# Causal attention over 32 groups with expert tiles between its scores: bursts of 4, 3, 3 banks, one block of value products, row maxima turned at full width and stacks loaded one group at a time

## The reference, cut to what matters

```python
q = (x @ wq).reshape(bsz, seq_len, N_HEADS, HEAD_DIM)
k = (x @ wk).reshape(bsz, seq_len, N_KV_HEADS, HEAD_DIM)
v = (x @ wv).reshape(bsz, seq_len, N_KV_HEADS, HEAD_DIM)
...
scores = jnp.einsum('bqhd,bkhd->bhqk', q, k) / np.float32(np.sqrt(HEAD_DIM))
scores = scores + mask
attn = jax.nn.softmax(scores.astype(jnp.float32), axis=-1).astype(q.dtype)
out = jnp.einsum('bhqk,bkhd->bqhd', attn, v).reshape(bsz, seq_len, N_HEADS * HEAD_DIM)
...
y_all = jax.nn.relu(jnp.einsum('bsd,edh->bseh', x, W_e) + b_e)
```

## Time and profile before

| | |
|---|---|
| runs of before | 664.77, 665.72, 666.27 us, median 665.72 |
| profiled execution | span 663.2 us; the page gives no time around it |
| PE busy in the span | 627.2 us (95%) |
| DVE busy in the span | 552.0 us (83%) |
| stretch from T of group 2 (137.80) to T of group 31 (543.09) | 405.3 us for 29 groups, 13.98 each |

### The profile page before, as it was taken

The page is one execution under the profiler, slowest core; times in us unless marked ns, Lnnn a source line. Parts: engine busy times, 40 slices in busy tenths (PEclk is TensorE's granted clock), DMA queues, the critical chain, the costliest instruction groups (busy, mean ns, idle before and its releaser), DMA issues.

```text
span 663.2 us, 12226 instructions
## 1 busy us (share of the span) xinstructions
PE 627.2 (95%) x3565; PEld 338.9 (51%) x3565; DVE 552.0 (83%) x1788; ACT 287.0 (43%) x535; POOL 238.2 (36%) x364
## 2 busy tenths in 40 slices
PE   8999999998999999999999999999999999789997
PEld 5788784433433334433443344443444343478886
DVE  6698999869978888989888798897789975689994
ACT  4353325434434435444444444443455443444441
POOL 3777641333323212332221322322222115576620
PEclk9999999969989999999999999999999999899999
DMA  7599989889788564675954649667276527768842
GB/s 262 141 336 266 337 239 173 146 164 273 152 268 161 166 139 80 154 132 188 194 105 98 136 109 220 125 173 152 52 167 111 171 72 241 156 145 217 217 104 79
DMA packets 79902, 113.10 MB, mean 171 GB/s; under 512 B 9704, under 2 KB 42664, under 8 KB 79840
## 3 DMA queue, kind: packets, MB, share of 16 engines
q1 hardware_dynamic: 68098, 86.90, 53.5%
q0 software_dynamic: 6704, 18.62, 11.8%
q10 hardware_dynamic: 5038, 6.84, 4.2%
HBM read 72.15 MB, written 39.65 MB: 169 GB/s over the span
## 4 chain that ended last, share of the span: by engine, by line
PE 55%; DVE 25%; DMA 8%; issue 4%; SPq 3%; POOL 2%; ACT 1%; ACTq 0%; DVEq 0%; POOLq 0%
PE bank L1672 13%; DVE bank L1390 12%; PE bank L1023 8%; PE bank L1591 7%; PE bank L2162 6%; PE bank L1644 5%; PE bank L1683 4%; PE bank L2167 4%; DMA w_e<-expert_rows,slots 3%; PE bank L1617 3%; DVE arena L1390 2%; DMA qt<-arena 2%; DMA qt<-turned_parts 2%; DVE m_parts L1403 2%; DVE m_parts L1405 1%
## 5 line engine op out<-in xcount | busy, mean ns | idle before, releaser
L1390 DVE CUSTOM_DVE_ANT_0 bank<-bank,cst 128x384 f32<-128x384 f32 (+3 forms) x512 | 234.9, 521 | 47.6 <-PE bank L1591 44.5
L1514 ACT ACTIVATE arena<-bank 128x512 f32<-128x512 f32 x320 | 170.9, 599 | 180.2 <-PE bank L1617 149.7
L1332 POOL TENSOR_SCALAR_AFFINE_SELECT arena<-arena 128x512 f32<-128x512 f32 x128 | 80.7, 643 | 309.2 <-ACT arena L1514 309.2
L1672 PE MATMUL bank<-w_e,arena 128*128 x312 | 162.2, 626 | 0.0
L1591 PE MATMUL bank<-kt,qt 48*128 48x512 f32 (+1 forms) x496 | 111.0, 338 | 5.6 <-DVE arena L1390 5.0
L1591 PEld LDWEIGHTS bank<-kt,qt 48*128 48x128 f32 x496 | 70.1, 187 | 83.9 <-DVE arena L1390 51.7
L1617 PE MATMUL bank<-qt,kt 50*128 50x512 f32 x256 | 88.2, 452 | 2.4 <-DMA qt<-arena 2.0
L1644 PE MATMUL bank<-arena 128*32 128x512 f32 (+3 forms) x1024 | 84.8, 445 | 0.4 <-ACT arena L1514 0.4
L1672 PEld LDWEIGHTS bank<-w_e,arena 128*128 128x128 f32 x312 | 54.6, 193 | 58.0 <-issue 54.3
L1390 DVE DVE_READ_ACCUMULATOR2_ANT arena<- 128x1 f32 x512 | 71.9, 140 | 0.0
L1683 PE MATMUL bank<-w_proj,arena 128*128 128x512 f32 x128 | 67.6, 636 | 0.0
(11 more groups left out here) (167 smaller groups left out, 942.7 us busy)
## 6 DMA issues: line engine op xcount, KB each, us to landing
qt<-turned_parts SPq DMA_DIRECT2D x96, 128.0 KB, 4.7
turned_parts<-qk_parts SPq DMA_DIRECT2D x8, 1280.0 KB, 7.2
gathered_rows<-s_tok SPq DMA_DIRECT2D x39, 256.0 KB, 5.3
arena<-gathered_rows SPq DMA_DIRECT2D x39, 256.0 KB, 3.4
expert_rows<-arena SPq DMA_DIRECT2D x39, 256.0 KB, 4.5
w_e<-in_L_ffn_W_e ACTq DMA_DIRECT2D x24, 256.0 KB, 6.2
kt<-turned_parts SPq DMA_DIRECT2D x96, 64.0 KB, 4.4
arena<-in_L_attn_x SPq DMA_DIRECT2D x16, 256.0 KB, 6.1
```

The source lines that it names most:

```text
L1332: g.affine_select(out=diag, in_=diag, compare_op=ALU.is_ge, fill=0.0, base=0, pattern=[[0, 2], [0, HALF], [1, P]], channel_multiplier=-1). ...
L1390: i = v.tensor_tensor_reduce(out=part, in0=part, in1=const("mask")[:, S - w:], scale=1.0, scalar=LOWEST, op0=ALU.add, op1=ALU.max, accum_o ...
L1514: nc.scalar.activation(pt[:, s, first:second + 1:second - first].rearrange("p c r q -> p c (r q)"), s2_bank(b, h, n).rearrange("p (c x) -> ...
L1672: i = t.matmul(bank[7], xgt[:, m % 2, k * P:(k + 1) * P], w_e[:, ex[m], k, :], start=False, stop=(k == KB - 1))
```

## The change

1. Four gaps instead of five; the quarters stand 2, 2, 2 or 2, 4, 2 or 4, 2, 2, and none in the last gap. TensorE's list of a group is now: scores 3 to 6 of the next group beside 0 to 3 of this one, gap 0, scores 7 to 9 beside 4 to 6, gap 1, T, scores 0 to 2 of the group after the next beside 7 to 9, gap 2, all four value products.
2. The row maxima are not split first. One copy puts them, twice, into the first two eighths of each half of `m_cols` (128 x 128, the rest zero from the start); T turns all 128 columns into bank 4; VectorE then makes the high part of the turned rows (a copy of 128 x 128) and, with a constant column that is -1 on the low rows and 0 elsewhere, high and low part in one more instruction. The constant rows of `kt` are -1 instead of 1. T also waits for `rows_of` of the last group, and the first value product for the read of bank 4.
3. Both row DMAs are issued by SP.
4. `load_stack` brings one group's stack with eight DMAs, four groups ahead of the group in work (before: twelve for two groups, three ahead).
5. `turns()` places `expert_x` by a new rule. In the groups 3 to 29 it stands at the first place of a group five times (18 times before) and twice at the second place of nine groups (never before).

```diff
-GAPS = 5
+GAPS = 4
-SIX, EIGHT = (2, 1, 1, 1, 1), (2, 2, 1, 1, 2)
+SIX, MIDDLE, FRONT = (2, 2, 2, 0), (2, 4, 2, 0), (4, 2, 2, 0)
-SIZES = [NONE, (0, 0, 0, 2, 2)] + [SIX, EIGHT] * 12 + [SIX, SIX] + [SIX, EIGHT, (2, 2, 1, 1, 0), NONE]
+SIZES = [NONE, (0, 0, 2, 2)] + [SIX, MIDDLE, SIX, FRONT] * 6 + [SIX, SIX] + [SIX, MIDDLE, SIX, NONE]
...
-        t = first[m] - 2 + m if m < 2 else max(first[m] - 2, last[m - 2])
-        t += -1 if t % 2 == 0 and (m < 2 or t > last[m - 2]) else t % 2 == 0
...
+        free = last[m - 2] if m > 1 else GAPS
+        slots = [t for t in range(free, first[m]) if t % GAPS in (1, 2)]
+        t = max([t for t in slots if t < first[m] - 1] or slots)
...
+    put("less", -1.0 * (p // 8 % 8 == 1))
...
-            if due(at := nth_of(NJ, b, h, -2 * NJ)):
+            if due(at := nth_of(NJ, b, h, -3 * NJ)):
                 e.wait_ge(b_s2, at)
...
-            for s in range(2):
-                for piece, (of_q, of_k) in enumerate(((0, 0), (0, 1), (1, 0))):
-                    at = 64 * s + HD * piece
-                    if (b, h) != (0, 0):
-                        e.dma_start(kt[at:at + HD, buf].bitcast(F32), k_rows[of_k]).then_inc(b_ld[buf], 16)
-                    e.dma_start(qt[at:at + HD, buf].bitcast(F32).rearrange("i g r t -> i g (r t)"), q_rows[of_q, s]).then_inc(b_ld[buf], 16)
+            for s in range(2):
+                at = 64 * s
+                if b or h > 1:
+                    e.dma_start(keys[at:at + 2 * HD].bitcast(F32), k_rows).then_inc(loaded, 16)
+                    e.dma_start(keys[at + 2 * HD:at + ROWS].bitcast(F32), k_rows[0]).then_inc(loaded, 16)
+                e.dma_start(queries[at:at + HD].bitcast(F32).rearrange("i r t -> i (r t)"), q_rows[s, 0]).then_inc(loaded, 16)
+                e.dma_start(queries[at + HD:at + ROWS].bitcast(F32).rearrange("i r t -> i (r t)"), q_rows[s]).then_inc(loaded, 16)
...
+        def maxima_columns(e, b, h):
+
+            e.wait_ge(b_m, nth_of(NJ, b, h, NJ))
+            rows = row_max.rearrange("p (s r) t -> p s (r t)", s=2)
+            nc.vector.tensor_copy(m_cols[:, :, 0:2], rows.unsqueeze(2).to_broadcast([P, 2, 2, HALF * TPB])).then_inc(b_mx, 1)
...
-            nc.vector.tensor_copy(m_rows, S1_BANK[nth_of(NJ, b, h, NJ + 2) % 3][0:2 * 2 * HALF * TPB, 0:P]).then_inc(b_me, 1)
+            v.tensor_copy(m_high[:, :], turned_at(b, h)).then_inc(dve_steps, st.one())
+            e.wait_ge(dve_steps, st.count())
+            v.scalar_tensor_tensor(out=m_rows[:, :], in0=m_high[:, :].bitcast(F32), scalar=const("less"), in1=turned_at(b, h),
+                                   op0=ALU.mult, op1=ALU.add).then_inc(b_me, 1)
...
-                    if b * NG + h + 1 < NB * NG:
-                        maximum_rows(e, *next_group(b, h, 1), 1)
-                    for n in (8, 9):
-                        exps(e, b, h, n)
-                    results(b, h, 3, 4)
+                    results(b, h, 2, 3)
...
-                    scores(e, (2, 3, 4), following, (0, 1, 2), (b, h))
+                    scores(e, (3, 4, 5, 6), following, (0, 1, 2, 3), (b, h))
                     quarters(b, h, 0)
-                    scores(e, (5, 6, 7), following, (3, 4, 5), (b, h))
+                    scores(e, (7, 8, 9), following, (4, 5, 6), (b, h))
                     quarters(b, h, 1)
-                    scores(e, (8, 9), following, (6, 7), (b, h))
-                    values(e, b, h, 0)
+                    turn_maxima(e, *following)
+                    scores(e, (0, 1, 2), after, (7, 8, 9), (b, h))
                     quarters(b, h, 2)
-                    turn_maxima(e, *following)
-                    scores(e, (0, 1), after, (8, 9), (b, h))
+                    for j in ORDER:
+                        values(e, b, h, j)
                     quarters(b, h, 3)
-                    for j in ORDER[1:]:
-                        values(e, b, h, j)
-                    quarters(b, h, 4)
...
-                        maximum_rows(e, *next_group(b, h, 1), 0)
-                    if h % 2 and b * NG + h + 3 < NB * NG:
-                        load_stacks(e, *next_group(b, h, 3))
+                        for s in range(2):
+                            maximum_rows(e, *next_group(b, h, 1), s)
+                    if b * NG + h + 4 < NB * NG:
+                        load_stack(e, *next_group(b, h, 4))
```

More of the change, by code:

```diff
@@ L77, in times_of @@
 def times_of(k):
-    return {UNITS[n][1]: 4 * (b * KV + h) + min(gap, 3) for (b, h, gap), quarters in WORK.items() for n, q in quarters
+    return {UNITS[n][1]: GAPS * (b * KV + h) + gap for (b, h, gap), quarters in WORK.items() for n, q in quarters
             if q == k and UNITS[n][0] == "x"}
@@ L121 @@
 for _name, _n in (("ident", P), ("half", 1), ("eps", 1), ("minus", 1), ("mask", S), ("tri", P), ("cos", TPB * 8), ("sin", TPB * 8), ("s4", 16),
-                  ("lower", E * E), ("i128", NT), ("i128m", MT + 1), ("tile", MT), ("iota", P), ("tilenum", TOPK * NT), ("part", 1), ("sel", E)):
+                  ("lower", E * E), ("i128", NT), ("i128m", MT + 1), ("tile", MT), ("iota", P), ("tilenum", TOPK * NT), ("part", 1), ("sel", E), ("less", 1)):
     COLS[_name] = (_at, _at + _n)
@@ L460, in sp_a @@
                         load_first(e)
-            load_stacks(e, 0, 0)
+            for h in (0, 1):
+                load_stack(e, 0, h)
         def dve_a(e, st):
@@ L466, in dve_a @@
             v.memset(be3[:, :], 0.0).then_inc(dve_steps, st.one())
+            v.memset(m_cols, 0.0).then_inc(dve_steps, st.one())
             e.wait_ge(a_load, 16)
@@ L622, in dve_a @@
                 maxima(e, 0, 1, n)
-            maxima_parts(e, st, 0, 1)
-            maxima_rows(e, 0, 1)
+            maxima_columns(e, 0, 1)
+            maxima_rows(e, st, 0, 1)
             dve_experts(e, st)
-            for n in (0, 1):
+            for n in (0, 1, 2):
                 maxima(e, 0, 2, n)
@@ L1070, in pe_a @@
                 values(e, 0, 0, j)
-            scores(e, (0, 1), (0, 2), (), None)
+            scores(e, (0, 1, 2), (0, 2), (), None)
             keep_awake(6, bank[2])
@@ L1207, in build @@
         row_max = take([P, R, TPB])
-        m_parts = parts("m_parts", [P, 2, 2, HALF * TPB], "arena", used[0])
-        take([P, 2, 2, HALF * TPB])
-        m_rows = take([P, P])[0:2 * 2 * HALF * TPB]
+        m_cols = take([P, 2, 8, HALF * TPB])
+        m_high = parts("m_high", [P, P], "arena", used[0])
+        take([P, P])
+        m_rows = parts("m_rows", [P, P], "arena", used[0])
+        take([P, P])
         rsum = take([P, QB])
@@ L1371, in build, with first_half, turned_at @@
         LOWEST = -3.0e38
-        def first_half(n):
-            return (n + 1) % 2, n // 2
+        def first_half(b, h, n):
+            return (n + (b * NG + h < 2)) % 2, n // 2
+        def turned_at(b, h):
+            return bank[(0, 1)[h] if b * NG + h < 2 else 4][:, 0:P]
         def maxima(e, b, h, n):
             v = nc.vector
-            s, kind = first_half(n)
+            s, kind = first_half(b, h, n)
             if n == 0 and due(at := nth_of(1, b, h, 0)):
@@ L1465, in go @@
                     if following:
-                        for n in (2, 3, 4):
+                        for n in (3, 4, 5, 6):
                             maxima(e, *following, n)
@@ L1472, in go @@
                     if following:
-                        for n in range(5, NJ):
+                        for n in (7, 8, 9):
                             maxima(e, *following, n)
-                        maxima_parts(e, st, *following)
+                        maxima_columns(e, *following)
                     for m in TURNS.get((b, h, 0), ()):
@@ L1478, in go @@
                     if following:
-                        maxima_rows(e, *following)
+                        maxima_rows(e, st, *following)
                     if after:
-                        for n in (0, 1):
+                        for n in (0, 1, 2):
                             maxima(e, *after, n)
@@ L1576, in scores_1 @@
             elif n == 0:
[L1577 to L1580 removed]
+                e.wait_ge(b_ld[h % 4], 16 * LOADS * (2 * b + h // 4 + 1) - (16 * LOADS // 2 if h % 4 < 2 else 0))
+            if n == 2 and b == 0 and h in (1, 2):
+                e.wait_ge(b_me, h)
             if (b, h) == (0, 1) and n == 0:
@@ L1819, in sp_b @@
                 load_expert(e, x)
-            load_stacks(e, 0, 2)
+            for h in (2, 3):
+                load_stack(e, 0, h)
             for b in range(NB):
```

61 lines of the change are left out of this document (24 added, 37 removed).

## The result

The changed kernel takes 708.4 us (median of 4 runs, 706.7 to 710.8) where the kernel before takes 665.25 beside it: 1.065 of before, 95% interval 1.062 to 1.069. The prediction was 664.1, range 654 to 673. It was wrong by 44 us.

The account below looks back on a forecast made before the run. PE was taken to set the pace, busy 388.0 of 405.3 us, with DVE 60 us to spare. The terms -20.9, -3.4, +16.8, +9.9 and -4.0 sum to -1.6 us, so 665.7 becomes 664.1 us, range 654 to 673.

Parts of the forecast that it names:

- item 5: Stack loads: eight issues a group instead of twelve in two, and a longer lead; worth nothing, SP's queue has room.
- Item 6: Both row DMAs on SP, one behind the other: the second lands in time unless queues are full; counted as 0.
- rival B: Slower, chance 0.25: rows, issued behind store and expert tiles, come too late for `scores_2(0)`; 9 us, 670 in all with 6.
- the landing of the rows sets the bursts: Sign that the prediction is wrong: row DMAs' landing, not the fourth bank's wait for maxima, sets the bursts; no size given.
- Rows as releasers of `scores_2(0)`: Sign in the new profile, at the head of the burst of four, that would show the rival with late rows.
- The lead-in "at nothing": Before T of group 2: one more row DMA on its chain, a shorter way to T; counted at nothing with the tail.
- The tail "at nothing": Behind T of group 31: a quarter and a value product more, fewer ahead; counted at nothing with the lead-in.
- rival D: Slower, chance 0.10: DVE's work behind T is longer; PE holes of 2 us or more in groups 3, 4, 21 lower the clock.
- Items 1 to 4: PE's work -20.9 us, wait at T -3.4, fourth bank of a burst +16.8, DVE late there +9.9, scores' old waits -4.0.
- item 2: T's wait for maxima falls from 14.1 to 10.7 us, -3.4; loads before a shape change always idle 0.76.

Follow-up runs that it names:

- E5: Changed kernel, still eight stack transfers a group, but with the 16 rows as outermost dimension and the 2 parts inside; 669.2 us, 1.006 of before.
- E3: Kernel before, its twelve stack transfers for two groups replaced by the changed kernel's eight for each group, at the same place; 840.1 us, 1.262 of before.
- E2: Changed kernel with the loads of before: two groups at once in 12 transfers of 16 partitions, three groups ahead; 703.7 us, 1.059 of before.
- E12: Kernel before with only its stacks loaded per group, four groups ahead, in 8 transfers with the rows outermost; 662.4 us, 0.994 of before.
- E9: E5 with row transfers ahead of gap 1's store and the expert tiles behind groups 11 and 19 alone; 666.3 us, 1.000 of before.
- E10: E5 with the nine doubled `expert_x` split, one at a place, the first of each pair one place earlier; 662.3 us, 0.995 of before.
- E7: Changed kernel, keys' 32-partition transfers (64 KB, 2 a group) kept, queries' cut in two of 16; 670.9 us, 1.008 of before.
- E1: Changed kernel, each stack transfer of 32 partitions cut in two of 16, so 12 transfers a group instead of 8; 670.8 us, 1.007 of before.

## Why the prediction was wrong

**The step that failed is item 5.** It said "eight DMA issues a group instead of twelve in two groups" and "more lead is worth nothing". It counted transfers and did not read their shape. Four of the eight have an outermost dimension of 2 and 3 updates each instead of 16, and while only a load's transfers moved the DMA share was 0.12, two of the 16 engines. Setting that right brings back 39 us of 43 (E5), and doing it to the kernel before costs 175 us (E3). "More lead is worth nothing" was read from a row of before (0.2 us of waiting for stacks), and that row does not show how little room there was: before, the last update of a load came less than 0.7 us ahead of the next T, or behind it, in 9 of 15 loads. With the old lead and the old pairs the new order takes 704 us (E2), since its load starts later behind T and its groups are shorter. Which of the two harms, and whether the longer lead was needed once a load lands in 7 us, is open. And in the old order loading per group is worth 4 us (E12), which the prediction had at nothing too.

**Item 6, counted as 0, and rival B** had the right place and a wrong reason. One of the prediction's own signs of being wrong, that the landing of the rows sets the bursts, came true. Rows as releasers of `scores_2(0)` are in the profile, 21.6 us on PE, also in plain groups like 13, where B has none. B's mechanism (issue behind the store and tiles) is real and is worth 2.4 us once landings are sound (E9). B was priced at a landing of 3.7 us, which no row shows; the 5.47 us of the earlier trace rows would have given (3.2 + 5.47 - 5.9) x 7 = 19 us, and its second term, 0.4 x 5, is 0.2 x 5 by its own numbers. The 5.47 us row was read as a full queue. A landing time depends on the shapes in flight (the same row transfer lands 5.4 us behind its issue in group 13 of the changed kernel and 2.0 in E5), and the change had altered these.

**The lead-in "at nothing"** cost 15.7 us, for the same cause: E5's T of group 2 stands at 137.0, 0.8 us ahead of before. **The tail "at nothing"** is 2.7 us longer in E5 (122.8 against 120.1), with the gathers of expert weights on its chain from 9.6 us behind T of group 31 on, 7.8 before. This was not tested by itself.

**The clock** (rival D's second half). In the stretch the granted clock is 0.96 where before has 0.99; of 430.9 us that is some 13 us more lost. It is at 0.5 of full speed in eight separate stretches of 3.4 us, besides one that T of group 2 stands in, as in every kernel here. Five of the eight begin within 2.5 us behind a wait of `scores_2(0)` for rows (0.80 to 4.05 us long), one (185.9) behind a wait of 2.06 us for maxima in a burst of four, two (274.7 and 387.3) behind a wait of T of 1.57 us for maxima. In E5, with nearly none of the waits for rows, there are two, behind waits of 2.38 and 1.79 us for maxima in groups 3 and 21, two of the three that D had named. So most of it is a second cost of the same cause: PE's waits for rows (16.6 us in the stretch against 2.5 in all of E5) and the clock (4% of 430.9 against 2% of 405.0, 9 us) make 23 of the 25.9 us between the changed kernel and E5. D, and with it the range up to 673, counted up to 1.7 us for each such stretch. No run shows this term by itself: it is an estimate, half of the 3.4 us at 0.50 that the earlier trace rows has once, behind 1.32 us of idle time on PE.

**Items 1 to 4 held**, and with the loads repaired the forecast is nearly met: E5's stretch is 405.0 against 405.3 before, where the sum said -1.6. (E5's trace is of an execution of 666.6 us; the median of its runs is 669.2, 5 over the forecast.) In single terms, from E5's order of time: `scores_2(0)` at T + 5.37 (said 5.37); the last pair of the burst of four 1.35 behind the first (said 1.34), the burst 1.78 us (said 1.77); groups with six quarters 12.4 (said 12.4), the h = 0 groups 13.7 (12.4 + 1.37), those with eight 13.8 to 14.5 where nothing disturbs them (said 13.7 and 14.1). T's weight load idles 29.5 us (said 33). (The 0.76 us of the earlier trace rows is in the trace of before the least idle time of a load of scores or values behind quarters, 116 of them; in front of quarters behind scores the median is 0.15, so item 2's "always" holds for the first alone.) The split of the rows takes 0.59 us from T's read to the next maximum (said 0.61). The bursts of four are 64.8 - 51.3 = 13.5 us over their 29 x 1.77; 2.5 of that are the two waits for rows, which leaves 11.0 for the lateness of VectorE (said 9.9). E10 shows that the doubled `expert_x` makes 3.7 of it.

## What to carry to other kernels

Before a load is called equivalent, read the outermost dimension of both its access patterns, not its bytes or its count: 2 there held the DMA share at 0.12, two of the 16 engines, with 192 KB a group for each of them by that reading, and 16 there with the same bytes brought back 39 of the 43 us (E5). It shows in a trace as updates of the semaphore per transfer (3 instead of 16) and as other transfers that land late in places that were not touched. And no wait in the old order does not mean that there is room: work out when a tile is wanted, when its buffer is free and how long its load takes to land, in the new order, before the row of the old one is believed.

## What the runs showed that was not expected

- The harm is not in proportion to the bytes: 64 KB a group on each of the two engines cost nothing (E7), 192 KB cost 38 us (changed kernel against E1), and 384 KB in one go every second group 175 us (E3). The last landing comes 9.0, 13.2 and 22.0 us behind the first issue, and a group lasts 12.4 to 14.1. In E3 the stacks themselves are waited for (145.2 us); in the changed kernel's stretch they never are, and what is late are the other transfers.
- A transfer of 16 x 2 x 1024 for two groups is dearer than the same bytes loaded per group: with the same bytes the hardware queue's packets took 53.5% of the engines' span before and 43.7% in E12, and the median to landing of the stores of gathered rows fell from 5.3 to 3.6 us. A packet of 4096 bytes took 433 ns before and 413 in E2, both with pairs, and 173 in E12 and 196 in E1, both without (medians). Why is not shown.
- A wait of PE can cost twice: itself, and then up to 1.7 us more, which is an estimate: half of a stretch of 3.4 us at 0.5 of the clock. Five of the changed kernel's waits for rows had such a stretch behind them; others, like the 1.38 us of group 13, had none.
